# Segment sums of a graph layer: each tile's product added to its block by VectorE, in place of sums of four tiles in PSUM

## What is computed

```python
def _L0_gnn_ref(node_feats, edge_feats, W, b, gamma, beta, edge_index):
    z = jnp.concatenate([node_feats[src], node_feats[dst], edge_feats], axis=1)
    z = z @ W.T + b
    mean = jnp.mean(z, axis=0)
    var = jnp.mean(jnp.square(z - mean), axis=0)
    z = (z - mean) * jax.lax.rsqrt(var + BN_EPS) * gamma + beta
    msg = jax.nn.sigmoid(z[:, :H]) * jax.nn.softplus(z[:, H:])
    agg = jnp.zeros_like(node_feats).at[src].add(msg)
    return node_feats + agg

edge_index = jnp.stack([src, dst])
x = _layernorm(x + _L0_gnn_ref(x, edge_attr_128, ..., edge_index), axis=-1)
x = _layernorm(x + _L1_gnn_ref(x, edge_index, ...), axis=-1)
```

## Time and profile before

| | us |
|---|---|
| median of 3 runs | 4397.55 |
| lowest, highest | 4392.38, 4400.34 |
| the profiled execution, its own time | 4391.44 |
| its span | 4389.2 |

### The profile page before, as it was taken

How to read it: one execution, slowest core, us unless ns; L and a number is a source line. 1 busy time by engine, 2 the same in 40 slices (tenths; PEclk the granted TensorE clock), 3 DMA queues, 4 the chain that set the end, 5 groups by cost and what they waited for, 6 DMA issues and landing times. The chain is left out here.

```text
span 4389.2 us, 80992 instructions
## 1 busy us (share of the span) xinstructions
PE 3005.1 (68%) x17430; PEld 2153.3 (49%) x17431; DVE 2808.1 (64%) x7053; ACT 2214.8 (50%) x5936; POOL 2540.0 (58%) x2618
## 2 busy tenths in 40 slices
PE   6866989999989999999996576666233333333341
PEld 3422444444457777777775465666233333333330
DVE  5898989999965545555553788888434344343457
ACT  2412989889866666666664999997100000000011
POOL 0787777777757777777774000000477777777750
PEclk8998999999999999999998789888655655565555
DMA  6333333333348888888888544442322222222240
GB/s 131 120 91 94 107 101 99 101 101 99 97 123 264 263 263 263 263 263 261 262 264 204 204 175 189 186 173 96 64 52 52 53 52 52 52 53 52 52 30 29
DMA packets 311349, 598.09 MB, mean 136 GB/s; under 512 B 53534, under 2 KB 191943, under 8 KB 305575
## 3 DMA queue, kind: packets, MB, share of 16 engines
q0 software_dynamic: 96992, 228.88, 20.5%
q1 hardware_dynamic: 175480, 246.10, 18.1%
q10 hardware_dynamic: 38736, 121.78, 7.3%
HBM read 406.57 MB, written 189.99 MB: 136 GB/s over the span
## 5 line engine op out<-in xcount | busy, mean ns | idle before, releaser
L345 POOL DMA_INDIRECT rec_d<-arena x830 | 846.7, 1020 | 392.7 <-issue 360.4
L1254 POOL DMA_INDIRECT arena<-x_tab,arena x880 | 834.1, 948 | 323.1 <-issue 278.2
L784 POOL DMA_INDIRECT arena<-b_tab,arena x880 | 832.7, 946 | 304.5 <-issue 256.9
L1266 PE MATMUL psum<-arena 128*128 128x129 f32 x1760 | 413.4, 428 | 730.5 <-DMA arena<-x_tab,arena 717.9
L1266 PEld LDWEIGHTS psum<-arena 128*128 128x128 f32 x1760 | 383.3, 330 | 760.4 <-issue 760.4
L1291 DVE TENSOR_TENSOR arena<-psum,arena 128x129 f32 x880 | 257.5, 293 | 673.0 <-PE psum L1266 553.6
L717 PE MATMUL psum<-arena 128*128 128x440 f16 x3360 | 663.6, 351 | 8.6 <-ACT arena L432 8.4
L805 DVE TENSOR_TENSOR arena<-psum,arena 128x512 f32<-128x512 f32 x440 | 283.4, 686 | 549.7 <-DMA arena<-b_tab,arena 280.3
L897 PE MATMUL psum<-weT,arena 128*128 128x256 f32 x1760 | 547.8, 393 | 53.7 <-DVE arena L805 50.4
L1242 ACT ACTIVATE arena<-l_idx 128x8 int32 (+1 forms) x110 | 22.9, 208 | 1079.1 <-DMA arena<-x_tab,arena 1069.4
L432 ACT ACTIVATE arena<-arena 128x128 f16<-128x128 f16 x1680 | 561.7, 386 | 0.0
(11 more groups left out here) (203 smaller groups left out, 5205.4 us busy)
## 6 DMA issues: line engine op xcount, KB each, us to landing
z_d<-arena ACTq DMA_DIRECT2D x220, 512.0 KB
arena<-z_d SPq DMA_DIRECT2D x44, 2560.0 KB, 8.5
arena<-rec_d SPq DMA_DIRECT2D x220, 260.0 KB
arena<-in_edge_attr SPq DMA_DIRECT2D x83, 640.0 KB
arena<-b_tab,arena POOLq DMA_INDIRECT x880
arena<-x_tab,arena POOLq DMA_INDIRECT x880, 2.5
rec_d<-arena POOLq DMA_INDIRECT x831, 2.6
b_tab<-arena ACTq DMA_DIRECT2D x49, 128.0 KB
```

The lines of the kernel that those rows point to most:

```text
L345: nc.gpsimd.indirect_dma_start(rec_rows, bass.IndirectOffsetOnAxis(e_idx[:, s, k:k + 1], 0), e_buf[:, s, k, :], None).then_inc(s_es[s], 16)
L784: nc.gpsimd.indirect_dma_start(bg[:, s, k, :], None, b_tab, bass.IndirectOffsetOnAxis(rec[:, s, k, H:H + 1].bitcast(I32), 0)).then_inc(s_b ...
L1254: nc.gpsimd.indirect_dma_start(xg[:, s, k, :], None, x1_tab, bass.IndirectOffsetOnAxis(gi[:, s, k:k + 1], 0)).then_inc(s_xg[s], 16)
L1266: last = nc.tensor.matmul(bank(4 * s + q)[:, a * 256:a * 256 + H + 1], hotg[:, s, 2 * q + a, :], xg[:, s, 2 * q + a, :], start=True, stop= ...
```

## The change

The sum of four tiles in PSUM is gone. Each tile's product goes to its own 128 columns of the bank, started afresh and not accumulated (`start=True, stop=True`), and VectorE adds each of the four to the block of its tile with an add of its own, 128x128. With this go the product of zeros, the read of the slots on TensorE, and the zero matrix. VectorE reads 20 block numbers for a chunk, in a row. `s_fl` now counts single adds: each of them waits for the one before it, and TensorE's group n waits for the last add of group n - 4 (`4 * n - 10`).

```diff
-        zerob = tmp([P], BF16)
...
                 def adds(c):
-                    _, firsts = nc.values_load_multi_w_load_instructions(
-                        blk_row[0:1, 0, :].rearrange("a (g k) -> a g k", k=YG)[:, bass.ds(c * CG, CG), 0], engines=[DVE_ENGINE], min_val=0, max_val=BLOCKS - 1,
+                    _, blocks = nc.values_load_multi_w_load_instructions(
+                        blk_row[0:1, 0, bass.ds(c * CG * YG, CG * YG)], engines=[DVE_ENGINE], min_val=0, max_val=BLOCKS - 1,
                         skip_runtime_bounds_check_because="the ids are clamped when made")
-                    return firsts
-
-                def add(c, j, g, first):
+                    return [blocks[g * YG:(g + 1) * YG] for g in range(CG)]
+
+                def add(c, j, g, blocks):
                     n, r = c * CG + g, ring(j, g)
                     wait(dve, s_sc, n + 1)
-                    wait(dve, s_fl, n + 2)
-                    dest = agg[:, bass.ds(first, YG), :].rearrange("p a f -> p (a f)")
-                    nc.vector.tensor_tensor(dest, bank(4 + r), dest, ALU.add).then_inc(s_fl, 1)
+                    for k in range(YG):
+                        wait(dve, s_fl, 4 * n + (k + 2))
+                        dest = agg[:, bass.ds(blocks[k], 1), :].rearrange("p a f -> p (a f)")
+                        nc.vector.tensor_tensor(dest, bank(4 + r)[:, k * P:(k + 1) * P], dest, ALU.add).then_inc(s_fl, 1)
...
                 def segment(c, j, g):
                     n, r = c * CG + g, ring(j, g)
-                    _, window = nc.values_load_multi_w_load_instructions(
-                        blk_row[0:1, 2, bass.ds(n * YG, YG)], engines=[PE_ENGINE], min_val=0, max_val=YG - 1,
-                        skip_runtime_bounds_check_because="every block has a tile, so four tiles in a row lie in four blocks in a row")
-                    wait(pe, s_fl, n - 1)
-                    nc.tensor.matmul(bank(4 + r), zerob, identb[:].unsqueeze(1).broadcast_to([P, YG, P]), start=True, stop=False, skip_group_check=True)
+                    wait(pe, s_fl, 4 * n - 10)
                     wait(pe, s_mc, n + 1)
                     wait(pe, s_hf, n + 1)
-                    slots = bank(4 + r).rearrange("p (w n) -> p w n", n=P)
                     for k in range(YG):
-                        last = nc.tensor.matmul(slots[:, bass.ds(window[k], 1), :].rearrange("p a n -> p (a n)"), hotf[:, g, k, :], msg[:, r, k * P:(k + 1) * P],
-                                                start=False, stop=(k == YG - 1), skip_group_check=True)
+                        last = nc.tensor.matmul(bank(4 + r)[:, k * P:(k + 1) * P], hotf[:, g, k, :], msg[:, r, k * P:(k + 1) * P], start=True, stop=True)
                     last.then_inc(s_sc, 1)
```

More of the change, by code:

```diff
@@ L933, in build @@
         msg = tmp([4, YG * P], F32)
-        zerob = tmp([P], BF16)
         s_zl = [sem(f"z_loaded{i}") for i in range(CS)]
-        (s_sig, s_q, s_v, s_lg, s_spl, s_msgT, s_hf, s_mt, s_mc, s_sc, s_fl, s_zw) = (
+        (s_sig, s_q, s_v, s_lg, s_spl, s_msgT, s_hf, s_mt, s_mc, s_sc, s_fl) = (
             sem(n) for n in ("sigmoid", "one_less_sigmoid", "v_scaled", "logs", "softplus", "messageT", "hot32",
-                             "message_transposed", "message_copied", "segment_product", "segment_added", "zero_weights"))
+                             "message_transposed", "message_copied", "segment_product", "segment_added"))
         def chunks(eng, step):
@@ L1037, in step @@
                         hots(c, g)
-                nc.vector.memset(zerob, 0.0).then_inc(s_zw, 1)
                 nc.vector.memset(agg[:, BLOCKS:BLOCKS + 3, :].rearrange("p b f -> p (b f)"), 0.0).then_inc(s_fl, 1)
@@ L1082, in step @@
                             segment(c - 1, (j - 1) % CS, g - LAG + CG)
-                pe.wait_ge(s_zw, 1)
                 chunks(pe, step)
```

## The result

The changed kernel takes 4578.31 us (median of 4 runs, 4577.07 to 4578.75) against 4397.37 us for the kernel before: a ratio of 1.0415 (95% interval 1.0399 to 1.0432), 181 us slower. The forecast was 4534 us with a range up to 4580: the direction is right, the time lies 1.7 us inside the end of the range, and of 181 us the forecast has 137: 44 us are missing.

The account below looks back on a forecast made before the run. ScalarE set the pace by a small margin; changed, VectorE would. Stage 9.6 + 752 + about 1 + 9.0 = 771.6 us, less 634.8 is +137; on the median 4397.55 that gives 4534 us, range 4512 to 4580.

Parts of the forecast that it names:

- The stage is the whole change: Only the message stage, 634.8 us or 14% of the span, changes; the kernel's time moves by what it moves.
- Add pitch 0.448 us, group 2.36, step 17.5: VectorE, message stage: dependent adds start 0.448 us apart, four adds with four one-hots take 2.36 us, a chunk's step 17.5.
- Rival A: VectorE's adds: waiting for the add before costs nothing, pitch 0.24 us, time 4397, no change; chance 5%.
- The table of 20 numbers is hidden: VectorE's load of 20 block numbers a chunk takes 1.5 us, hidden behind L1030's 2.75 us.
- Rival B: VectorE's load of 20 values isn't hidden: 2.0 us a step, 84 us more, 4618; chance 6%.
- TensorE keeps up: TensorE's products come in time even at its lower clock, so VectorE's 24.6 us of waiting for them go.
- Rival C: TensorE loses clock from 0.87 and sets the message stage's pace: 41 us more, 4575; chance 9%.
- rival D: Message stage: removing the zeroing products' 94 us shortens waits, time falls by up to 70 us to 4328; chance 1%.
- ScalarE keeps up: ScalarE's logarithm is ready 3.5 us before VectorE's next step; VectorE's 44 us of waiting for it go.
- The sum of 771.6 us: Message stage's predicted length: chunk 0, 43 steps, the uncovered load and the last adds total 771.6 us.
- the forecast's own range of 4515 to 4555: Kernel time if VectorE sets the pace with adds at 0.448 us, given 79%: 4515 to 4555 us.
- VectorE busy over 85%, ScalarE near 75%: Predicted sign in the message stage: VectorE busy over 85% of it, ScalarE near 75%.

Follow-up runs that it names:

- e2: Changed kernel with one one-hot behind each add instead of four behind four; 59.4 us slower than the kernel before, ratio 1.0099.
- e4: Kernel before with only VectorE's half of the change: four dependent adds, TensorE still clearing and summing in slots; 193.6 us slower than the kernel before, ratio 1.0338.
- e8: Kernel before with the scaled v made by GpSimd instead of ScalarE and a group's four one-hots by one comparison; ratio 0.9978 to the kernel before, -14.9 us.
- e7: Kernel before with the scaled v made by GpSimd instead of ScalarE; 23.6 us slower than the kernel before, ratio 1.0061.
- e6: Changed kernel with a group's four one-hots made by one comparison of 128x512; 104.1 us slower than the kernel before, ratio 1.0183.
- e9: Changed kernel with the scaled v made by GpSimd instead of ScalarE; 210.0 us slower than the kernel before, ratio 1.0479.
- e10: Changed kernel with 48 semaphore increments on VectorE ahead of its steps, moving the loop's code; 189.4 us slower than the kernel before, one run.
- e11: Changed kernel with 96 semaphore increments on VectorE ahead of its steps, moving the loop's code; 163.9 us slower than the kernel before, one run.
- e13: Changed kernel with each z load of the loop held back until L1027 of the chunk three before; 158.4 us slower than the kernel before, ratio 1.0362.
- e5: Kernel before with VectorE's loop running eight chunks a turn instead of four; 3.0 us slower than the kernel before, ratio 1.0003.

## Why the prediction was right, and what it missed

- *The stage is the whole change*: right, 184.5 us of the stage against 181 of the time.
- *Add pitch 0.448 us, group 2.36, step 17.5*: 0.433, 2.32 and 17.4 on average without the gaps. L1291's rows were the right price. e2 shows that it is a wait, e4 that VectorE's half of the change alone makes the loss.
- *Rival A, the wait costs nothing*: refuted by 0.43 us in the changed kernel; the sentence of the Trainium skill, "VectorE: DVE Perf Modes", section "The DRAIN you can't avoid", that the prediction names would have made it no change, and does not hold for these adds.
- *The table of 20 numbers is hidden*: it took 1.35 us (1.5 estimated) behind L1030, and the first add follows L1030 after 2.74 us as before. Rival B is out.
- *TensorE keeps up*: 1.8 us of waits, though the granted clock fell from 0.87 to 0.74. Rival C named the fall of the clock rightly and its cost wrongly; rival D is out by e4.
- *ScalarE keeps up*: it idles, as worked out (its second Sigmoid waits 91.8 us for L1027); VectorE waits for it at the first chunk only.
- *The sum of 771.6 us*: 819.3. **The term that was missing is the code of VectorE's loop.** The prediction's step of 17.5 us is added up from what the instructions take; I had the longer loop body before me and priced its work, not its loading. It costs 51 us here, nine turns of 5.7. The other terms came to 768.2, 3.4 us under the forecast. The mechanism of the adds was right. But that the measured time lies inside the range is luck: it lies 1.7 us from its upper end, 23 us above the forecast's own range of 4515 to 4555, and the width up there was meant for the cost of rival C, which didn't come.
- *VectorE busy over 85%, ScalarE near 75%*: 81% and 71%, by the same gaps.

## What to carry to other kernels

Sums in PSUM that let one wide add stand for several dependent narrow ones were worth far more here than the TensorE work they cost: 220 clearing products (94 us before, hidden) against 207 us more of VectorE's time for the adds (220 groups of 2.32 us instead of 1.38), which hid only as far as VectorE had waited before. Where dependent adds can't be avoided, put independent instructions between them; that gave back more than half of the loss with the same work. And count the instructions of a hand-written loop on each engine: ask the trace for packets on the instruction queue inside the stage, and for large loads issued near the backward branch.

## What the runs showed of the hardware

- Loops of 147 (e8), 266 (e7) and 267 (before) instructions on VectorE ran without any packet of instructions behind the backward branch; loops of 334 (e6), 439 (changed, e2, e4, e9, e10, e11, e13) and 531 (e5) had packets on every turn. Where between 267 and 334 it begins was not tried.
- The head of such a loop came 2.8 to 3.1 us after the backward branch, and 5.2 to 6.2 us where a load of 2560 KB had been issued 0.25 to 3.9 us ahead of the branch. e13 changed nothing but the time of these loads, and its gap went from long to short.
- The gaps cost 51 us (nine of 5.7) where VectorE set the pace, and some 0.3 us a turn where it was waiting for ScalarE anyway (e5).
- A VectorE add of 128x128 behind a wait for the one before it started 0.43 to 0.45 us after that one, though it takes 0.29; a one-hot between the two left the distance as it was (e2).
- A GpSimd tensor_scalar of 2560 columns held up a VectorE tensor_scalar beside it until it ended, 2.45 us at most for one of 0.28, and a tensor_tensor with both inputs in SBUF for 2.76 at most (e8). Adds with one input in PSUM kept their 0.29 us beside it (e9).
